# Two-layer gated cross-attention and expert network on one core: loads reordered over two queues, score planes repeated by their write transfers, router exponentials moved to POOL, new instruction orders

## The reference, cut to what matters

```python
x = x + tanh(g_xattn[0]) * L0_xattn(layernorm(x), ctx, ...)   # 16 heads of 8, strictly causal softmax
x = x + tanh(g_ffn[0])   * L0_ffn(layernorm(x), ...)          # top-1 of 6 experts, 100 tokens each
x = x + tanh(g_xattn[1]) * L1_xattn(layernorm(x), ctx, ...)   # 8 heads of 64, softmax over 256 keys
x = x + tanh(g_ffn[1])   * L1_ffn(layernorm(x), ...)          # top-2 of 8 experts per batch, then a norm
...
# L1_ffn: one router decision per batch
rw = softmax(x.mean(axis=1) @ Wr + br);  tk_w, tk_i = top_k(rw, 2);  tk_w = softmax(tk_w)
h = gelu(x_flat @ W1[e] + b1[e]);  expert_out = h @ W2[e] + b2[e]
```

## Time and profile before

| | us |
|---|---|
| median of three runs | 248.61 (246.94 to 249.54) |
| the profiled execution | 246.28 |
| span of its instructions | 244.6 |
| PE busy | 205.9 |
| DVE / ACT / POOL busy | 151.0 / 137.6 / 94.4 |

### The profile page before, as it was taken

One profiled execution on the slowest core, in us unless ns is written; L12 is line 12 of the kernel. 1 busy time (PEld: TensorE's weight loads), 2 busy tenths in 40 slices (PEclk: granted clock), 3 DMA queues, 4 the chain that ended last, 5 costly groups with the idle time before them and its releaser, 6 DMA issues.

```text
span 244.6 us, 4582 instructions
## 1 busy us (share of the span) xinstructions
PE 205.9 (84%) x1626; PEld 146.4 (60%) x1626; DVE 151.0 (62%) x384; ACT 137.6 (56%) x343; POOL 94.4 (39%) x140
## 2 busy tenths in 40 slices
PE   0587998869998899999869998999799995299990
PEld 0465555334454584776557867777566774299990
DVE  2355229846795846658896789649579636215643
ACT  4268541275838668377728485555787631725340
POOL 7450000034608229406950366747836712001111
PEclk9999599979999999999999999999999999589998
DMA  4918999600000000000000000000051600640000
GB/s 122 325 54 236 187 259 255 121 4 3 3 5 4 3 0 3 0 0 3 0 1 4 0 0 0 3 0 3 0 160 39 186 9 0 222 168 21 24 23 21
DMA packets 13770, 15.09 MB, mean 62 GB/s; under 512 B 1316, under 2 KB 11300, under 8 KB 13748
## 3 DMA queue, kind: packets, MB, share of 16 engines
q1 hardware_dynamic: 13316, 14.27, 21.8%
q10 hardware_dynamic: 432, 0.54, 0.8%
HBM read 11.00 MB, written 3.67 MB: 60 GB/s over the span
## 4 chain that ended last, share of the span: by engine, by line
PE 57%; DVE 21%; ACT 9%; POOL 5%; issue 3%; DMA 3%; SPq 1%; POOLq 0%; DVEq 0%; ACTq 0%
PE PS L1271 7%; DVE MX L735 6%; PE PS L1261 5%; ACT POOLED L620 4%; PE PS L1231 4%; PE PS L1202 4%; PE PS L1215 4%; PE PS L1179 4%; PE PS L1101 3%; PE PS L1039 3%; DMA CT<-in_ctxT 3%; DVE NM L832 2%; PE PS L1242 2%; PE PS L1188 2%; PE PS L1044 2%
## 5 line engine op out<-in xcount | busy, mean ns | idle before, releaser
L440 POOL TENSOR_TENSOR POOLED<-POOLED,RC 128x512 f32<-128x512 f32 x32 | 32.6, 1042 | 24.3 <-DVE RC L841 24.3
L735 DVE TENSOR_REDUCE MX<-PS 128x4 f32<-128x1024 f32 (+1 forms) x24 | 27.6, 1215 | 16.1 <-PE PS L1063 16.1
L620 ACT ACTIVATE POOLED<-PS,NM 128x256 f32<-128x256 f32 x64 | 29.5, 477 | 9.1 <-DVE NM L832 8.5
L429 POOL TENSOR_SCALAR_AFFINE_SELECT PT<-PT 128x512 f32<-128x512 f32 x16 | 10.2, 637 | 51.3 <-ACT PT L551 51.3
L551 ACT ACTIVATE PT<-PS 128x768 f32<-128x768 f32 x32 | 24.1, 809 | 10.5 <-PE PS L1082 10.5
L397 POOL TENSOR_SCALAR VE<-MV 128x2 f32<-128x2 f32 x20 | 5.1, 256 | 51.2 <-DVE MV L688 51.2
L1271 PE MATMUL PS<-POOLED 128*128 128x128 f32 x128 | 17.3, 293 | 5.0 <-ACT POOLED L662 5.0
L832 DVE TENSOR_REDUCE NM<-PS 128x4 f32<-128x1024 f32 x16 | 19.3, 1215 | 3.4 <-PE PS L1202 3.3
L1271 PEld LDWEIGHTS PS<-POOLED 128*128 128x128 f32 x128 | 16.9, 208 | 5.6 <-issue 5.3
L662 ACT ACTIVATE POOLED<-PS,BI 128x256 f32<-128x256 f32 x32 | 12.4, 479 | 13.8 <-PE PS L1261 13.8
L1202 PE MATMUL PS<-KT,VA 64*128 64x256 f32 x128 | 17.6, 399 | 2.1 <-ACT POOLED L620 2.0
(11 more groups left out here) (146 smaller groups left out, 444.6 us busy)
## 6 DMA issues: line engine op xcount, KB each, us to landing
POOLED<-in_w SPq DMA_DIRECT2D x8, 512.0 KB, 4.7
qk_scr<-POOLED SPq DMA_DIRECT2D x4, 768.0 KB, 7.0
POOLED<-qk_scr SPq DMA_DIRECT2D x8, 384.0 KB, 7.2
W<-in_w SPq DMA_DIRECT2D x1, 768.0 KB, 9.5
BI<-in_bias SPq DMA_DIRECT2D x8, 66.0 KB, 4.3
CT<-in_ctxT SPq DMA_DIRECT2D x2, 256.0 KB, 8.1
out_x<-X SPq DMA_DIRECT2D x4, 128.0 KB, 1.8
VEC<-in_vecs ACTq DMA_DIRECT2D x1, 324.5 KB, 6.5
```

Of the source, the lines that this page charges most:

```text
L440: g_.tensor_tensor(pr, pr, RC1[:, n % 2, 2 * h:2 * h + 2].unsqueeze(2).to_broadcast([P, 2, S]), ALU.mult).then_inc(s_p1p, 1)
L620: last = a.activation(PR[n % 3][:, h, it, :], pair("sc", n)[:, h * 512 + it * S:h * 512 + (it + 1) * S], ACT.Exp, bias=NM1[:, n % 2, 2 * h ...
L735: v.tensor_reduce(MX0[:, b, it, :, hw * k:hw * (k + 1)], pair("S", n).rearrange("p (r h j) -> p r h j", r=2, h=hw), AXX, ALU.max, negate=T ...
```

## The change

All five order tables are new. Beside them:

- Loads: SP now takes x and the context in pieces (one batch, one batch, two batches) with W0 between them. ACT's queue takes the identity, AB, the gates, WTD, COL and then the masks ahead of its first activation; the gate weights TG and two thirds of W1 (keys, values) are issued by ACT in the step `load`, behind its first value copy. The 649 vector entries and WO0 come from SP behind the ones rows, the query third of W1, WO1 and WR behind the last read of planes. Waits are made finer to match.
- Score planes: only six planes are kept in SBUF (three parts, two sides). `split_out(b, part)` writes each part as soon as it exists, one transfer per side, and the transfer itself repeats it. There are 24 such transfers where there were 4. ACT's `hd` and `md` copies are gone (12 instructions).
- Maxima rows: the eight transfers at line 359 are issued by ACT, right behind its copy.
- Router: both exponentials are a power of e on POOL. The first is an addition and a power, and the sum of eight comes by a reduction on DVE.
- The last matmuls: `eo:m` writes its two token tiles to two banks and signals each; for the second expert of a batch DVE adds and takes statistics tile by tile.

```diff
-            sp.dma_start(X[:, 0:2, :], xr[:, 0:2, :]).then_inc(d_x[0], 16)
-            sp.dma_start(X[:, 2:4, :], xr[:, 2:4, :]).then_inc(d_x[1], 16)
-            sp.dma_start(W0[:, :, :], w0).then_inc(d_w0, 16)
-            sp.dma_start(CT[:, 0:half], ctxT[:, 0:half]).then_inc(d_ctx[0], 16)
...
+            cut = (0, S, 2 * S, 4 * S)
...
+            load_x(0)
+            sp.dma_start(W0[:, :, :], w0).then_inc(d_w0, 16)
+            load_ctx(0)
+            load_x(1)
+            load_ctx(1)
+            load_x(2)
+            load_ctx(2)
...
+            def split_out(b, part):
+
+                sp.wait_ge((s_hi, s_mid, s_parts)[part], b + 1)
+                for side in range(2):
+                    sp.dma_start(qk_scr[b, side, PLANES[side][part]].rearrange("k p t -> p k t"),
+                                 SPLIT[b][:, 3 * side + part:3 * side + part + 1].to_broadcast(
+                                     [P, 3 - part, S])).then_inc(d_scr[b], 16)
...
+            def late(i):
+
+                if i == 0:
+                    sp.dma_start(VEC[:, V_BO0:NVEC], vecs[V_BO0:NVEC].partition_broadcast(P)).then_inc(d_vec, 16)
+                    sp.dma_start(WO0[:, :], wo0).then_inc(d_late, 16)
+                if i == 1:
+                    sp.dma_start(W1[:, 0, :], w1[:, 0, :]).then_inc(d_w1[0], 16)
+                    sp.dma_start(WO1[:, :, :], wo1).then_inc(d_late, 16)
+                    sp.dma_start(WR[:, :], wr).then_inc(d_late, 16)
...
+            def router_exp(b):
+
+                pool.wait_ge(s_lgr, b + 1)
+                link(g_.tensor_tensor(LX[:, b, :], LG[:, b, :], MR[:, b:b + 1].to_broadcast([P, NE]), ALU.add))
+                g_.tensor_tensor(ER[:, b, :], EXPB[:, :], LX[:, b, :], ALU.pow).then_inc(s_er, 1)
+
+            def second_exp(b):
+
+                pool.wait_ge(s_dd, b + 1)
+                g_.tensor_tensor(E2[:, b:b + 1], EXPB[:, 0:1], DD[:, b:b + 1], ALU.pow).then_inc(s_e2, 1)
...
-            act.dma_start(CST[:, :], consts).then_inc(d_c, 16)
+            act.dma_start(CST[:, 0:C_MASK], consts[:, 0:C_MASK]).then_inc(d_i, 16)
+            act.dma_start(AB[:, :], ab).then_inc(d_ab, 16)
             act.dma_start(VEC[:, 0:V_BO0], vecs[0:V_BO0].partition_broadcast(P)).then_inc(d_g, 16)
-            act.dma_start(VEC[:, V_BO0:NVEC], vecs[V_BO0:NVEC].partition_broadcast(P)).then_inc(d_vec, 16)
+            act.dma_start(WTD[:, :, :], wtd).then_inc(d_wtd, 16)
+            act.dma_start(COL[:, :], cols).then_inc(d_wt, 16)
+            act.dma_start(CST[:, C_MASK:NCONST], consts[:, C_MASK:NCONST]).then_inc(d_c, 16)
...
+            def load(i):
+
+                if i == 0:
+                    act.dma_start(TG[:, 300:306], wgate).then_inc(d_wtd, 16)
+                act.dma_start(W1[:, 1 + i, :], w1[:, 1 + i, :]).then_inc(d_w1[1 + i], 16)
...
                 a.activation(MT[:, b % 2, :], misc[0:32, 0:128].bitcast(bf16), ACT.Copy).then_inc(s_mt, 1)
+                act.wait_ge(s_mt, b + 1)
+                for r in range(2):
+                    act.dma_start(QK[64 * r + KR:64 * r + KS, 0, b, :].rearrange("k (h t) -> k h t", t=S),
+                                  MT[16 * r:16 * r + 16, b % 2, :]).then_inc(d_shift[b], 16)
...
+                    pe.wait_ge(d_wtd, 32)
...
                 for t in range(2):
                     for f in range(FT):
-                        last = mm(bank[:, t * P:(t + 1) * P],
+                        last = mm(bank[:, 512 * t:512 * t + P],
                                   HT[:, m % 2, f, t * P:(t + 1) * P], W12[m][:, F + f * P:F + (f + 1) * P],
                                   start=(f == 0), stop=(f == FT - 1))
-                last.then_inc(s_y, 1)
+                    last.then_inc(s_y, 1)
```

More of the change, by code:

```diff
@@ L63 @@
-tp:11 sc:14 av1:10 tp:12 sc:15 av1:11 tp:13 wo1:2 tp:14 av1:12 av1:13 tp:15 av1:14 av1:15 xT:3:2 hid:0 wo1:3
-hid:1 r1:2 xT:3:3 r1:3 eo:0 hid:2 eo:1 hid:3 eo:2 hid:4 eo:3 hid:5 eo:4 hid:6 eo:5 hid:7 eo:6 eo:7
+tok:0 xT:0:0 pk:0 pq:0 pk:1 xT:0:1 tok:1 pq:1 pk:2 xT:0:2 pq:2 pk:3 xT:0:3 tok:2 pq:3 kv:0:0 kv:0:1 kv:1:0 S:0
+S:1 S:2 kv:1:1 S:3 S:4 S:5 kv:2:0 S:6 S:7 mT:0 S:8 kv:2:1 S:9 T:0:0 S:10 T:0:1 S:11 T:1:0 T:1:1 T:2:0 S:12 T:2:1
+AV:0 mT:1 S:13 T:3:0 S:14 AV:1 T:3:1 S:15 hT:0 S:16 T:4:0 T:4:1 AV:2 AV:3 T:5:0 S:17 T:5:1 hT:1 AV:4 T:6:0 S:18
@@ L65 @@
+sc:4 sc:5 val:6 xT:2:2 av1:2 av1:3 sc:6 wo1:0 tp:4 sc:7 pte:7 q:2 val:7 tp:5 sc:8 tp:6 xT:3:0 sc:9 av1:4 av1:5
+tp:7 sc:10 r1:0 tp:8 sc:11 av1:6 av1:7 xT:2:3 tp:9 q:3 av1:8 tp:10 sc:12 sc:13 tp:11 wo1:1 sc:14 av1:9 tp:12
+sc:15 av1:10 av1:11 tp:13 wo1:2 av1:12 av1:13 xT:3:1 tp:14 r1:1 hid:0 tp:15 xT:3:2 av1:14 av1:15 r1:2 hid:1
+wo1:3 eo:0 eo:1 xT:3:3 hid:2 r1:3 hid:3 eo:2 eo:3 hid:4 hid:5 eo:4 eo:5 hid:6 hid:7 eo:6 eo:7
 """)
 ACT_ORDER = table("""
-v0c:0 xTc:0:0 v0c:1 hi:0 hd:0 xTc:0:1 md:0 hi:1 hd:1 xTc:0:2 v0c:2 v0c:3 md:1 kvc:0:0 xTc:0:3 hi:2 hi:3 hd:2
```

224 lines of the change are left out of this document (106 added, 118 removed).

## The result

The changed kernel takes 229.44 us (median of four runs, 228.84 to 231.86); the kernel before takes 247.98 on the same chip. The ratio is 0.927, 95% interval 0.918 to 0.935: 7.3% faster. The forecast was 232.0. The profiled execution took 229.93 with a span of 228.2, where the sum of the prediction had 229.6. So the total is met within half a microsecond, but each of its terms is off, by 0.4 to some 7 us, and they cancel. Some executions, whatever the kernel, fell into a slower state with a lower clock; ratios and their intervals leave these out, medians and ranges of times have them in.

What follows compares the result with a forecast made beforehand. PE bounds the kernel, working 205.9 of 244.6 us, so time is its work plus its idle and half-clock stretches. Terms -6.4 + 0.8 - 2 + 0 - 8.7 - 0.4 = -16.7 us gave 232 us, range 226 to 241.

Steps and rivals of the forecast that it cites:

- behind it: After the last `eo`: half the sum and statistics lies beside the last matmuls, -0.4 us of 5.5.
- The start: Up to the first score step: earlier loads bring `S:0` from 34.4 to 28 us, gain 6.4 (2.7 to 8).
- `xT:0:0` is ready by then: Start: first transposed x ready when ACT's second table load ends, about 7.3 us; its copy ends at 7.8.
- rival A: Start gives back half: `tok:1` waits 6 or 7 us, low clock for three `kv` steps; 236 us, chance 0.18.
- Two queues: Loads issued by SP and ACT: a second queue adds no bandwidth, only sharper order; start's gain stays 6.4 us.
- The maxima stage: Scores to transposed scores: moved work +0.8 us, waits and low clock closed for 2 us gained (0 to 4).
- a `d_shift` wait of over 2 us on PE: Sign in the new profile, PE waiting for the maxima rows, that would show the forecast wrong.
- The middle: Up to the last `av1`: same steps reordered, 10.5 us idle; gain taken as 0, 4 us either way.
- The end: Last `av1` to last `eo`: interleaved steps remove idle time and low clock, gain 8.7 us (6 to 9.4).
- B: Rival: new waits of 6 to 8 us among layer-1 heads or expert logits; 239 us, chance 0.14.
- C: Rival: small plane writes run one after another, making it slower than before; about 285 us, chance 0.04.
- D: Rival: middle's idle time shrinks by 4 to 5 us and start reaches its fast end; 226 us, chance 0.06.

Runs made afterwards that it cites:

- e1: Changed kernel with POOL's fill of VA put ahead of the first rstd again, as before; 230.54 us, ratio to the kernel before 0.933.
- e10: Changed kernel with the read of batch 3's planes held until the maxima rows of batch 1 have landed; 226.63 us, ratio to the kernel before 0.915.
- e8: Changed kernel with the step orders of before on PE, DVE, ACT and POOL, new loads, writes and exponentials kept; 258.11 us beside 248.1 before.
- e11: Changed kernel with batch 3's plane read behind batch 1's maxima rows and gate weights issued first in ACT's setup; 224.54 us, ratio to before 0.907.
- e9: The changed kernel itself, unaltered, run again in the last group; 230.56 us, ratio to the kernel before 0.934.
- e3: Changed kernel with SP's late weight loads held until the maxima rows of batch 1 have landed; 227.72 us, ratio to the kernel before 0.922.
- e7: Changed kernel with all six plane writes of a batch held until its last part exists; 227.28 us, ratio to the kernel before 0.912.

## Why the prediction was right, and where its steps failed

Against the profiled executions, the sum was -16.7 us, measured are -16.3 (246.28 to 229.93).

| term | forecast | measured |
|---|---|---|
| start, to `S:0` | -6.4 | -4.9 |
| `S:0` to the last `av1` (the 2.1 us of moved work taken off) | -1.2 | -4.4 |
| last `av1` to last `eo` | -8.7 | -7.1 |
| behind it | -0.4 | 0 |

The total is met by luck: the start, the maxima stage and the end fell short, and the middle, for which nothing was counted, paid for them.

**The start.** The size was off: 29.5 instead of 28, inside 26.5 to 31.7. The sentence that failed is "`xT:0:0` is ready by then": it gave nothing for POOL's fill beside `XH`, whose new place is in the kernel's order table, nor for `tok:0` in front of it, which held PE to 7.6 us. `hi:0` was 2.7 us late; the fill has 1.1 of them (10.90 in e1), the rest was there without it, `tok:0`, the table load, which ended at 8.43 and not at 7.3, and projections of 1.06 us where 0.60 was the later price. The wait for the gate weights was seen (2.53 us), its end 2.5 us later than forecast for these reasons. Behind it came what rival A had put at the `kv` steps, a low clock, 0.63 and 0.50 up to 20 us, and `pq:3` ended at 24.5 instead of 20.6. That `S:0` was late by 1.5 and not by 3.9 us is the three `kv` steps, which ran at 1.00 in 5.2 us where 28 had left them 7.4.

The Trainium skill, in "SBUF — State Buffer", section "SBUF: two separate sides", says that VectorE and GpSimd share a pair of ports, and that of two instructions that need the pair the one that starts first holds it for its whole length while the other blocks. The trace agrees: 0.60 us alone, 2.83 us beside the fill of 2.60, ending 0.14 us behind it. It is a rule that spoke against this change and that the prediction did not weigh. The like is seen later: the pair of `XH` takes 1.71 us at 161.56, beside POOL's divisions, and in all 18.5 us instead of the 11.9 before, 6.6 us of DVE time. For `XH` PE waited only 2.3 us in all, at three places.

**Two queues.** "No gain in bandwidth, only the sharper order" fits: up to `T:0:0` the shares are 0.69 to 0.86 and the rates 175 to 198 GB/s, where the kernel before had 0.74 and 186 up to its `S:0`. No run changes the queue of the first loads alone, so it isn't shown more closely.

**The maxima stage.** "I count 2 us gained (0 to 4)" failed: from 44 to 65 us PE was busy 15.3 of 21 us, in the kernel before, which was in the same stage, 18.2. The text named the cause, `T:0:0` late for the maxima rows, but took some 4 us for the whole way, with a landing as if the queues were empty. Behind planes and late loads the rows took 6.6 us, and it was `T:4:0` that paid most. By the forecast's own sign, a `d_shift` wait of over 2 us on PE, it is wrong here: the waits were 2.3 and 3.0 us. "DVE without a 5 us gap in the maxima stage" did not come either: the gap was 5.88 us, where the kernel before had 5.14. The price of the second, shown by e10, is 3.9 us by the medians and 2.6 us between the profiled executions.

**The middle.** "All of it gone, or as much again; I take 0" was wrong by about 7 us: PE idles 3.6 us between 61.1 and 191.6. This paid for the start, the maxima stage and the end. No run takes this apart, so its cause stays open; that e8, with the old orders, lost the whole gain speaks for the order of the steps, no more.

**The end.** Right in its mechanism and nearly in size. The copy of heads, the gelu table and the first gelu were done in time, and PE's waits there are one of 0.93 us, for the norm of batch 3, and seams. The forecast of 29.6 us was 31.2: the one wait, and the steps themselves, busy 30.1 us where 28.9 were added up. The power of 8 elements, taken at 1.5 us, took 1.64, that of one 0.55 to 0.73. The stretch of low clock went with the idle time, as forecast.

**The rivals.** A (the start gives back half) was true for a quarter, with the low clock at other steps; B (the middle pays) was not. C (writes one after another) is out: the 24 writes landed after 1.8 to 6.4 us each, by the median 3.5, with the last issued at 49.2; they overlap, for they were issued within 36.6 us. D came nearest on the middle, "shrinks by 4 to 5", where it was 7, but not on the start; that e10 has 226.6 us, near D's 226, comes from the maxima rows and not by D's conditions.

## What to carry to other kernels

When transfers are spread over time and queues, list the small ones that a matmul waits for and ask what bulk is under way when they are issued: 8 KB behind 768 KB and beside 516 KB took 6.6 us, 4.6 without the 516, and at most 1.4 us ahead of both. A start made faster pays only if the next wait moves with it; e1 gained 2.8 us at `S:0` and nothing in the time, e11 gained in both. And before a difference between two traces is put down to an edit, compare the granted clock of the stretch: of e1's 2.8 us at `S:0` only about 1 was the edit. In e10 the clock was higher behind the wait and no higher over the whole stage.

## What the runs showed of the hardware

- A fill by POOL of 128x2944 (2.60 us) held a DVE instruction pair of 0.60 us for 2.83 us.
- The granted clock was 0.66 from 60 to 65 us behind a PE gap of 3.0 us (changed, e9). It was 0.66 from 50 to 55 us too, some 5 us behind a gap of 2.3 us with one of 0.7 and one of 1.1 in between.
- Behind gaps of 3.6 and 3.1 us at `T:0:0` it was 0.50 from 45 to 50 us (e3, e11), and from 55 us on 0.99 or more, though `T:4:0` waited 1.0 us or `S:18` 0.6. With a gap of 0.7 us at `T:0:0` it was 1.00 from 40 to 75 us (e7).
- The same start gave 0.67 and 1.00 from 15 to 20 us in two kernels (changed, e3), and `S:0` at 29.5 and 27.7. What decides between the two isn't shown.
